# A tile's quarters widened from 125 to 128 columns, and the gate's scales turned by VectorE in 32x32 squares

## The reference, cut to what matters

```
x: [10000, 128]   adj: [10000, 10000]   E = 8 experts, H = 256
h   = item_feat @ W_item.T + b_item
x   = x + relu(adj @ h + layernorm(x) @ W_user.T + b_user)
xf  = layernorm(x)
p   = softmax(xf @ gate_w + gate_b)            # [N, 8]
cw  = p where p is one of the row's two largest, else 0
out = x + sum over e of cw[:, e] * (gelu(xf @ W1[e] + b1[e]) @ W2[e] + b2[e])
```

## Time and profile before

| | |
|---|---|
| median of 3 runs | 1627.0 us |
| the profiled execution, its own time | 1627.57 us |
| its span, from first to last instruction | 1625.8 us |
| busy: TensorE matmul / VectorE / ScalarE / GpSimd | 98% / 92% / 78% / 5% |
| mean busy share of the DMA engines by SyncE's queue | 84.4% |
| granted TensorE clock, mean over the span | 0.997 |

### The profile page before, as it was taken

How to read it: one execution, slowest core, us unless ns; L and a number is a source line. 1 busy time by engine, 2 the same in 40 slices (tenths; PEclk the granted TensorE clock), 3 DMA queues, 4 the chain that set the end, 5 groups by cost and what they waited for, 6 DMA issues and landing times.

```text
span 1625.8 us, 26954 instructions
## 1 busy us (share of the span) xinstructions
PE 1600.5 (98%) x7325; PEld 1323.4 (81%) x7325; DVE 1487.9 (92%) x2324; ACT 1265.7 (78%) x1637; POOL 86.1 (5%) x63
## 2 busy tenths in 40 slices
PE   7999999999999999999999999999999999999997
PEld 6878888888888888888888888888888888888875
DVE  6988999898999999999999899999998989898986
ACT  5777878777878787878787787878787878777865
POOL 2000000000000000000000000000000000000000
PEclk9999999999999999999999999999999999999998
DMA  9999888989898989898989898988989898889842
GB/s 358 345 326 308 280 307 283 305 270 315 270 314 268 315 267 315 270 313 276 316 282 303 283 301 291 291 291 290 301 279 312 275 308 281 306 274 309 275 155 64
DMA packets 148974, 467.05 MB, mean 287 GB/s; under 512 B 16837, under 2 KB 44518, under 8 KB 148954
## 3 DMA queue, kind: packets, MB, share of 16 engines
q1 hardware_dynamic: 144776, 459.00, 84.4%
q10 hardware_dynamic: 3346, 5.51, 0.9%
q0 software_dynamic: 832, 2.30, 0.4%
HBM read 461.30 MB, written 5.44 MB: 287 GB/s over the span
## 4 chain that ended last, share of the span: by engine, by line
issue 91%; PE 3%; POOL 2%; DMA 1%; DVE 1%; ACT 1%; POOLq 0%; ACTq 0%; DVEq 0%
POOL rstd_sb L394 2%; DMA raw<-in_adj_main 1%; PE acc L784 0%; PE acc L785 0%; ACT g_sb L484 0%; PE acc L786 0%; DVE g_lo L683 0%; DMA w_item_sb<-in_w_itemT 0%; ACT a_hi L432 0%; DVE a_lo L574 0%; DVE o_sb L706 0%; PE ps_v L755 0%; PE ps_y L813 0%; PE ps_z L855 0%; PE ps_z L853 0%
## 5 line engine op out<-in xcount | busy, mean ns | idle before, releaser
L432 ACT ACTIVATE a_hi<-raw 128x1000 fp32r<-128x1000 f32 (+1 forms) x800 | 811.1, 1027 | 241.9 <-PE acc L786 183.0
L574 DVE TENSOR_TENSOR a_lo<-raw,a_hi 128x1000 fp32r<-128x1000 f32 x780 | 913.6, 1194 | 71.3 <-ACT a_hi L432 69.9
L784 PE MATMUL acc<-a_hi,h_hi 128*128 128x500 f32 x1560 | 611.6, 392 | 5.3 <-DVE a_lo L574 4.4
L786 PE MATMUL acc<-a_hi,h_lo 128*128 128x500 f32 x1560 | 606.8, 389 | 0.0
L785 PE MATMUL acc<-a_lo,h_hi 128*128 128x500 f32 x1560 | 604.7, 388 | 0.0
L784 PEld LDWEIGHTS acc<-a_hi,h_hi 128*128 128x128 f32 x1560 | 293.3, 188 | 64.0 <-issue 6.8
L786 PEld LDWEIGHTS acc<-a_hi,h_lo 128*128 128x128 f32 x1560 | 293.3, 188 | 59.5
L785 PEld LDWEIGHTS acc<-a_lo,h_hi 128*128 128x128 f32 x1560 | 293.8, 188 | 57.9
L484 ACT ACTIVATE g_sb<-ps_z,b_sb 128x500 f32<-128x500 f32 x320 | 198.0, 670 | 37.2 <-PE ps_y L815 29.8
L683 DVE TENSOR_TENSOR g_lo<-g_sb,g_hi 128x500 fp32r<-128x500 f32 x320 | 201.9, 672 | 22.8 <-ACT g_hi L490 22.8
L490 ACT ACTIVATE g_hi<-g_sb 128x500 fp32r<-128x500 f32 x320 | 179.2, 611 | 0.0
(11 more groups left out here) (125 smaller groups left out, 926.7 us busy)
## 6 DMA issues: line engine op xcount, KB each, us to landing
raw<-in_adj_main SPq DMA_DIRECT2D x780, 500.0 KB, 5.2
spread_sb<-scales SPq DMA_DIRECT2D x160, 250.0 KB, 6.9
xr_sb<-in_xR SPq DMA_DIRECT2D x20, 250.0 KB
x_sb<-in_xT SPq DMA_DIRECT2D x20, 250.0 KB, 4.3
out<-o_sb ACTq DMA_DIRECT2D x20, 250.0 KB, 5.9
items<-in_itemT SPq DMA_DIRECT2D x13, 384.0 KB, 8.3
raw<-in_adj_rem SPq DMA_DIRECT2D x20, 156.2 KB, 5.6
g_sb<-in_w POOLq DMA_DIRECT2D x4, 250.0 KB, 6.7
```

The source lines that it names most:

```text
L432: nc.scalar.activation(a_hi[q][0:rows, 0:cols], raw[s][0:rows, 0:cols], ACT.Copy).then_inc(hi_ready, 1)
L574: nc.vector.tensor_tensor(low, whole, val(high), ALU.subtract).then_inc(lo_ready, 1)
L784: nc.tensor.matmul(acc[:, 0:T], w_hi, m_hi, start=(k == 0), stop=False)
L786: last = nc.tensor.matmul(acc[:, 0:T], w_lo, m_hi, start=False, stop=False)
```

## The change

A quarter becomes 128 columns wide (the four cover 512, of which the last 12 are zero): `x1_sb` and `xn_sb` get 12 more columns, cleared once at the start; `xr_sb` is loaded on 128 partitions from an input padded with zero rows; every operation on [125, ...] becomes one on [128, ...]. VectorE writes `cw_sb` in the order (expert, quarter), so that it is [128, 32], and turns it at once with one `transpose`, which turns each 32x32 square by itself, into `cwT_sb` [128, 32]. TensorE's four transposes (T_TRANS), the semaphore `cwT_done` and ScalarE's copy (A_SPREAD) are gone. ScalarE's store stays at p = 28 and writes `cwT_sb` by an access pattern that puts the squares' rows in place: 128 pieces of 32 numbers in place of 8 rows of 500. The loads of `spread_sb` are as they were.

```diff
-TQ = T // Q
+TQ = P
+TW = Q * TQ
+SQ = 32
-T_TURN, T_BACK, T_GATE, T_TRANS = 1, 9, 13, 24
+T_TURN, T_BACK, T_GATE = 1, 9, 13
-        x1_sb = sb("x1_sb", [P, T])
+        x1_sb = sb("x1_sb", [P, TW])
-        xn_sb = sb("xn_sb", [P, T])
+        xn_sb = sb("xn_sb", [P, TW])
-        cwT_sb = sb("cwT_sb", [E, T])
+        cwT_sb = sb("cwT_sb", [P, SQ])
-        scales = nc.dram_tensor("scales", (E, T), fp32).ap()
+        scales = nc.dram_tensor("scales", (E * Q, TQ), fp32).ap()
+        scales_of = scales.rearrange("(e q) t -> e (q t)", q=Q)
...
-                                 scales[e].partition_broadcast(P)).then_inc(...)
+                                 scales_of[e, 0:T].partition_broadcast(P)).then_inc(...)
...
-                if p == A_SPREAD:
-                    act.wait_ge(cwT_done, i)
-                    since(act, cw_stored, i * 16 - 16)
-                    nc.scalar.activation(cwT_sb[:, :], ps_g[0:E, 0:T], ACT.Copy).then_inc(cwT_ready, 1)
                 if p == A_SEND:
                     act.wait_ge(cwT_ready, i)
                     since(act, scaled, expert(i, 0))
-                    act.dma_start(scales, cwT_sb[:, :]).then_inc(cw_stored, 16)
+                    act.dma_start(scales.rearrange("r (b j) -> b r j", j=SQ), cwT_sb[:, :]).then_inc(cw_stored, 16)
...
+            nc.vector.memset(x1_sb[:, T:], 0.0)
+            nc.vector.memset(xn_sb[:, T:], 0.0)
...
-                    nc.vector.scalar_tensor_tensor(out=cw_sb[:, :], in0=rank_sb[:, :], scalar=1.5, in1=prob_sb[:, :],
-                                                   op0=ALU.is_lt, op1=ALU.mult).then_inc(cw_ready, 1)
+                    nc.vector.scalar_tensor_tensor(out=cw_sb.rearrange("p (e q) -> p q e", q=Q), in0=quarters(rank_sb[:, :], E),
+                                                   scalar=1.5, in1=prob, op0=ALU.is_lt, op1=ALU.mult).then_inc(cw_ready, 1)
+                    dve.wait_ge(cw_ready, i)
+                    since(dve, cw_stored, i * 16 - 16)
+                    nc.vector.transpose(cwT_sb[:, :], cw_sb[:, :]).then_inc(cwT_ready, 1)
...
-                if p == T_TRANS:
-                    pe.wait_ge(cw_ready, i)
-                    for q in range(Q):
-                        last = nc.tensor.transpose(ps_g[0:E, q * TQ:(q + 1) * TQ], cw_sb[:, q * E:(q + 1) * E],
-                                                   ident_sb[0:TQ, 0:TQ])
-                    last.then_inc(cwT_done, 1)
...
+    rows = _np.zeros((NB, TW, D), _np.float32)
+    rows[:, :T] = x.reshape(NB, T, D)
-        "xR": x.reshape(NB, Q, TQ, D).transpose(0, 2, 1, 3).reshape(NB, TQ, Q * D),
+        "xR": rows.reshape(NB, Q, TQ, D).transpose(0, 2, 1, 3).reshape(NB, TQ, Q * D),
```

More of the change, by code:

```diff
@@ L92 @@
 W_SPLIT = 16
-A_RELU, A_NORM, A_XN, A_EXP, A_SPREAD, A_SEND, A_STORE, A_USER, A_FFN, A_SCALED = 2, 13, 15, 17, 27, 28, 30, 38, 4, 6
+A_RELU, A_NORM, A_XN, A_EXP, A_SEND, A_STORE, A_USER, A_FFN, A_SCALED = 2, 13, 15, 17, 28, 30, 38, 4, 6
 V_X1, V_STATS, V_NORM, V_LO, V_USTATS, V_UNORM, V_SCALED = 2, 4, 6, 12, 10, 31, 6
@@ L253, in build @@
         cw_ready = sem("cw_ready")
-        cwT_done = sem("cwT_done")
         cwT_ready = sem("cwT_ready")
@@ L351, in spread @@
                     sp.dma_start(spread_sb[e % SPREADS][:, :],
-                                 scales[e].partition_broadcast(P)).then_inc(spread_landed[e % SPREADS], 16)
+                                 scales_of[e, 0:T].partition_broadcast(P)).then_inc(spread_landed[e % SPREADS], 16)
             def one_pass(i, with_finish):
@@ L448, in user @@
                     act.wait_ge(u_turned, i + 1)
-                    nc.scalar.activation(xn_sb[:, :], ps_x[:, 0:T], ACT.Copy).then_inc(u_kept, 1)
+                    nc.scalar.activation(xn_sb[:, 0:T], ps_x[:, 0:T], ACT.Copy).then_inc(u_kept, 1)
             def tail(i, p):
@@ L462, in tail @@
                     act.wait_ge(xn_lo_ready, i)
-                    nc.scalar.activation(xn_sb[:, :], ps_x[:, 0:T], ACT.Copy).then_inc(xn_ready, 1)
+                    nc.scalar.activation(xn_sb[:, 0:T], ps_x[:, 0:T], ACT.Copy).then_inc(xn_ready, 1)
                 if p == A_EXP:
@@ L619, in tail @@
                     since(dve, added, expert(i, 0) - (E - 1))
-                    nc.vector.tensor_tensor(x1_sb[:, :], x_sb[:, :], r_sb[:, :], ALU.add).then_inc(x1_ready, 1)
+                    nc.vector.tensor_tensor(x1_sb[:, 0:T], x_sb[:, :], r_sb[:, :], ALU.add).then_inc(x1_ready, 1)
                 if p == V_STATS:
@@ L705, in add @@
                         dve.wait_ge(added, expert(i, e))
-                    nc.vector.tensor_tensor(o_sb[:, :], x1_sb[:, :] if e == 0 else o_sb[:, :], t_sb[e % 2][:, :],
+                    nc.vector.tensor_tensor(o_sb[:, :], x1_sb[:, 0:T] if e == 0 else o_sb[:, :], t_sb[e % 2][:, :],
                                             ALU.add).then_inc(added, 1)
@@ L802, in user @@
                     pe.wait_ge(u_kept, i + 1)
-                    nc.tensor.matmul(acc[:, 0:T], w_user_sb[:, :], xn_sb[:, :], start=False, stop=False).then_inc(u_dense, 1)
+                    nc.tensor.matmul(acc[:, 0:T], w_user_sb[:, :], xn_sb[:, 0:T], start=False, stop=False).then_inc(u_dense, 1)
             def down(i, e):
```

## The result

| | before | after |
|---|---|---|
| median of 6 runs | 1626.86 us | 1616.72 us (1616.22 to 1618.61) |
| profiled execution, span | 1627.57, 1625.8 us | 1616.59, 1614.8 us |
| matmul of the last adjacency step (L775, now L779), first | 88.70 us | 87.16 us |
| from there to the next (pass 1) | 70.85 us | 69.95 us |
| each of the 18 later passes | 78.434 us | 78.153 us |

The account below looks back on a forecast made before the run. TensorE's own instructions were taken to bound each pass. 1627.57 - 8.4 + 0.3 + 0.7 - 1.3 - 1.5 = 1617.4 us for the profiled execution, 0.6 less for the median: 1616.8; eight in ten between 1612.5 and 1623.

Parts of the forecast that it names:

- TensorE's transposes: At step 24 of passes 1 to 19: removing four transposes saves 0.44 us a pass, 8.4 us in all.
- The wider operations: Remaining transposes and gate, three columns wider: cost 0.015 us a pass (0 to 0.03), 0.3 us in all.
- VectorE's turn: After `cw_sb` in each pass: the new transpose takes 0.2 us, hidden; VectorE's pass grows to at most 73.7 us.
- The store and SyncE: Scales' store to first broadcast: room 4.7 us, store 4.9, SyncE 0.2 late; 0.04 us a pass, 0.7 in all.
- The cover behind SyncE: At step 37 of a pass: VectorE is done 0.67 us before TensorE begins, room for late loads.
- Rival 1: Late store makes SyncE hold adjacency loads; slower from a 5.9 to 6.0 us store, 1646 us at 7; chance 0.16.
- rival 2: In the passes: loads, not TensorE, set the pass, so 8.1 us of gain are lost, 1624.2 us; chance 0.08.
- The end: Last tile's chain from `cw_sb` through the store to the scaling: 1.3 us less, ends 0.4 and 1.5.
- rival 4: Last tile's low clock stays away or lasts twice as long: about 2 us either way; variant within the forecast's 0.76.
- The start: Load of `xr_sb` on 128 partitions no longer delays `raw` behind it: 1.5 us less, from 0 to 2.2.

Follow-up runs that it names:

- no_turn: The kernel before without TensorE's four transposes and ScalarE's copy, zeros stored as the scales; 1616.86 us, ratio 0.9939.
- wide_te: The kernel after with its quarters of 128 columns, but TensorE's four transposes and ScalarE's copy kept; 1628.19 us, ratio 1.0007.
- layout: The kernel before with `x1_sb` and `xn_sb` only allocated 12 columns wider, moving what lies behind them; 1628.95 us, ratio 1.0016.
- turn125: The kernel after with quarters of 125 columns, the store in two DMAs, every tensor at its address of before; 1617.16 us, ratio 0.9934.
- late_send: The kernel after with the store of the scales two steps later, at step 30 in place of 28; 1668.54 us, ratio 1.0252.
- send29: The kernel after with the store of the scales one step later, at step 29 in place of 28; 1625.31 us, ratio 0.9993.
- rows128: The kernel before with only `xr_sb` loaded on 128 partitions from a padded input; 1624.75 us, ratio 0.9987.

## Why the prediction was right, and where it was off

The total was right: 1616.8 predicted, 1616.72 measured, and most of its mechanisms held. Four of its terms were off, one by +3.0 us and three by -0.7, -0.7 and -2.2, and nearly cancel; that is luck. For the profiled execution it said 1617.4; 1616.6 was measured.

- **TensorE's transposes.** 0.44 us a pass from one detour in the timeline; 0.453 measured by no_turn. Right, by the method of comparing the distance of the two matmuls around the detour with an ordinary one.
- **The wider operations.** 0.015 us a pass, bounds 0 and 0.03; wide_te shows 0.173. This is the step that failed. Its own part is 0.03, the upper bound. The rest lies on matmuls that the change doesn't touch: 0.09 through the addresses of tensors allocated behind the widened ones (layout), 0.05 unexplained. In all 19 passes 3.0 us more than the term had. The bounds came from what three more columns cost in the operations themselves, and the term put what the wider tensors do to the other matmuls at nothing, without a word on it.
- **VectorE's turn.** 0.2 us taken, 0.21 measured, hidden as said: 17 of turn125's 18 passes equal no_turn's, and VectorE's pass of 73.5 us is within the 73.7.
- **The store and SyncE.** Room 4.7 us, measured 4.72; store 4.9, measured 4.98 on average up to the broadcast, waiting included; SyncE 0.2 late, measured 0.35. But the 0.7 us charged for it were not lost: TensorE has no wait for an engine in the passes after. The cover behind SyncE was read as 0.67 us from one step of one pass; late_send and send29 put it at about 2 on average, with 0.7 in the one pass of turn125 that lost time. Rival 1 was the right danger with too near a limit: with 2 us of cover and gains of 0.57 a pass, slower begins at a store of about 7.3 us (an estimate: 4.7 + 2 + 0.57) and not 5.9. send29 shows how near it lies: one step of delay, 2 us more of SyncE's waiting, and the gain cannot be told from nothing.
- **The loads as the bound (rival 2).** ScalarE's wait for `raw` fell in place of growing. Wrong, for the reason given against it.
- **The end.** 1.3 predicted, 0.4 to 1.5 as ends. The chain gave 1.7 in the trace, a little beyond the upper end, and 1.5 in no_turn, where the clock falls as before. The low part of g starts 0.38 us behind the start of `cw_sb`; within 0.5 was said. The other 1.8 us of the profile after is rival 4's effect in the favourable direction: 1.8 against its "about 2".
- **The start.** 1.5 predicted, 2.2 at most. In the kernel after 1.5 came before the first last-step matmul, as predicted, and 0.6 in pass 1, which layout and no_turn gained without the new load; rows128's medians give 2.2 for both. The wait behind the load was 1.45 us, as read, though not the longest: that is the 1.48 at 13.8 us, which stayed. On 128 partitions the view gives a landing time, as the prediction read from its absence; on how many DMA engines the load runs no view shows. The Trainium skill's rule in "DMA: Bandwidth & Descriptors", section "Why a DMA increments its semaphore by 16 and not by 1", gives 5 engines for 125 rows and 16 for 128. The trace after agrees for `xr_sb`, with its landing time of 5.3 us and the wait of 1.45 us that went. For the store the same rule spoke against the change, and here too the measurement goes its way: its last packet ended 4.3 us behind the issue in place of 3.2, and in the last tile, without the adjacency's loads, there are 1.97 us from the store to the first broadcast in place of 1.44. But the pieces are also 128 in place of 8, and no run separates the two.

The sum, corrected: 1617.4 + 3.0 (width) - 0.2 (transposes) - 0.7 (SyncE) - 0.7 (start and pass 1) - 2.2 (last tile, 1.8 of it the clock) = 1616.6. So the fit of the middle value is partly chance: without the clock's share this execution would have taken about 1618.4, 1.0 above the sum and inside the range.

## What to carry to other kernels

Take the price of an instruction on the bound engine from the distance between its neighbours, and test it by leaving it out. When a tensor gets wider, allow for the addresses behind it: here 0.1 us in a pass of 78, on instructions that nobody edited; a pad keeps them where they were, as in turn125, whose passes took what no_turn's did. And before a semaphore is moved onto a queue that also carries the loads, find how late that queue may be, by delaying it on purpose: here about 2 us on average, and one step of delay cost the whole gain.

## What the runs showed of the hardware that was not expected

- Moving tensors by 32 or 64 bytes in SBUF changed the mean distance of TensorE's matmuls, group by group, by between -2.2 ns (`ps_y<-g_hi,w_lo`, 227.5 to 225.3) and +1.9 (`ps_y<-g_hi,w_hi`, 225.7 to 227.6), alike in 17 of 18 passes; together 78.434 to 78.524 us. How is open: `acc<-a_hi,h_lo`, whose operands did not move, went from 226.9 to 227.6 ns.
- The 16 KB store of the scales, cut into four DMAs, was seen later by SyncE than as one (its wait 10.6 us in all against 5.2): ScalarE issues the fourth 1.33 us behind the first.
- In the last tile, where TensorE is idle in part, the granted clock is low for 6.8 us in some traces, 3.4 in others, and not at all in two until the last 4 us, and `cw_sb` comes up to 1.8 us later for it. Executions of one kernel differ as well: the kernel before ran at a mean clock of 0.994 to 1.0 and took 1625.6 to 1630.9 us. That is half of what this change gained, so stages before the last tile are the better measure of it.
